# Two buffers for each set of raw expert weights, shared experts first, routing weights before the indexed stores

## Chip, core and metric

One core of a Trainium2 chip runs the whole kernel. The metric is the device time of one execution in microseconds. The engines are TensorE (PE in the rows, its weight loads PEld), VectorE (DVE), ScalarE (ACT), GpSimd (POOL) and SyncE (SP), which only issues DMAs here.

## What is computed

The input `x` is (2, 1024, 128) in float32: 2048 tokens of 128 channels. An attention block comes first, then a mixture of experts; each has a layer norm before it, a layer norm behind it, and adds its result to `x`. The part that the change touches is the second block:

```
rw = _route(x, gate_w, gate_bias)             # 8 of 64 experts a token, from 4 of 8 groups
expert_out = vmap(_mlp)(Wg, Wu, Wd)           # _mlp: silu(x @ gw.T) * (x @ uw.T) @ dw.T, inner width 88
routed = einsum('eth,te->th', expert_out, rw)
shared = _mlp(x, Sg, Su, Sd)                  # inner width 176
out = routed + shared
```

## The kernel before

The 2048 tokens are four quads of 512. The expert layer treats them in two ways. Quads 2 and 3 (`DENSE`) go through all 64 experts: the 64 x 88 inner rows are cut in 11 rounds of 4 sets of 128 rows (8 rows of each of 16 experts), and a step is one set with one quad. Its six products form gate and up from weights and activations split in a high and a low part (`x_hi`, `x_lo`, `w_hi`, `w_lo`), ACT makes the silu in place, DVE multiplies up by the token's routing weight (`weigh`, L1295) and by the gate (`hidden`, L1305), and one more product (`down`, L1762) adds into the quad's PSUM bank. Quads 0 and 1 (`SPARSE`) are sorted by expert instead: GpSimd writes each token's row to eight slots of a DRAM table `pair_x` with 64 indexed stores of 128 rows (`scatter`, L732; a stage `I` is two of them), TensorE works through the table in a burst of 64 units after round 4, and 64 indexed reads (`gather`, L741) bring the results back during rounds 5 to 10. The shared expert is two steps for each quad, the second one (`is_rest`) of only 48 rows.

The first 16 steps (`FIRST`) are the eight shared ones and round 0. Every engine has a hand-written order of stages for them, `PE_ORDER`, `ACT_ORDER`, `DVE_ORDER` and `POOL_ORDER`, and works strictly in it. The letters that matter: `Z` a step (its gate and up on PE, its silu on ACT, its products on DVE), `D` its down product, `E` and `F` input and routing logits of a quad, `H`, `J`, `I`, `O`, `M` on DVE the choice of groups and experts and the sum of the weights, `M` on POOL the routing weights (`write_route`, L817), `G` and `N` their transpose and their spreading over the 128 rows of a set (L1713, L1728), `X` and `Y` the counting that gives the slots, `R` the split of a set of weights. On POOL `I` is a stage of indexed stores.

Raw expert weights arrive in `w_raw`, one buffer a set. ACT copies the high part (`split_hi`, L985), DVE subtracts for the low part (L1371), and the down product reads the raw buffer. So the next load of a set may be issued only when the last down product of its last round is done:

```
sp.wait_ge(s_whi, n + 1)
wait_w_lo(sp, n)
sp.wait_ge(s_down, last_user(n) + 1)
sp.dma_start(w_raw[:, c, :], w_experts[r, c]).then_inc(s_wl[c], 16)
```

SP issues these loads in order (wait at L619, load at L620), and after each of the first ones three of the 38 late loads (`gu_w`, `down_w`, L604) that the burst needs. A step may begin on PE when the hidden product of the step two before it is done (`s_hid`). PE tells the others of its results by `s_gate`, `s_up` and `s_down`, one increment each a step.

Of the kernel before, what the change touches and what calls it, by code (L numbers as in the profile page):

```python
# [41 lines left out]
P = 128  # L42
# [12 lines left out]
def build(nc, x, w_basis_t, w_v, b_v, w_o_t, b_o, gate_w_t, gate_bias, w_experts, w_shared_up,  # L55
# [39 lines left out]
    with ExitStack() as ctx:  # L95
# [32 lines left out]
        up_w = sb("up_w", [P, 2, 512])  # L128
        y_t = sb("y_t", [P, QUADS, 512])
        x_hi = sb("x_hi", [P, len(DENSE) * 512], F32R)  # L130
        x_lo = sb("x_lo", [P, len(DENSE) * 512], F32R)
        route_w = sb("route_w", [P, SETS, len(DENSE) * 512])
        w_raw = sb("w_raw", [P, SETS, 3 * P])
        w_hi = sb("w_hi", [P, SETS, 2 * P], F32R)
# [81 lines left out]
        down_w = sb("down_w", [HID, E, C])  # L216
        pair_in = sb("pair_in", [P, 4, 4, C])
        pair_xt = sb("pair_xt", [P, 2, 2 * P])
        pair_g = sb("pair_g", [P, 2, UNIT_TILES, HID])
        pair_h = sb("pair_h", [P, 2, UNIT_TILES, HID])  # L220
        pair_ht = sb("pair_ht", [HID, 2, 2 * P])
        pair_out = sb("pair_out", [P, 4, UNIT_TILES, C])
        picked = sb("picked", [P, 3, CHOSEN, C])
# [57 lines left out]
        s_rw = sem("route_w_ready")  # L281
        s_wl = [sem(f"expert_w_loaded{k}") for k in range(SETS)]
        s_shl = sem("shared_w_loaded")
# [78 lines left out]
        def stages(names):  # L362
# [16 lines left out]
        )  # L379
        DVE_ORDER = stages(  # L380
# [4 lines left out]
        )  # L385
        POOL_ORDER = stages(
            "B0 S1 P1 S2 P2 S3 D0 K0 P3 X0 R0 D1 R1 R2 F0 X1 L0 L1 E0 J0 D2 M0 F1 X2 J1 E1 D3 "
            "X3 F2 M1 E2 J2 R3 E3 I0 I1 M2 F3 I2 I3 J3 I4 I5 I6 M3 "
            + " ".join(f"I{n}" for n in range(7, 32))
        )  # L390
# [50 lines left out]

        FIRST = [(q, c, False) for q in SPARSE for c in range(SHARED)]
        for q in DENSE:
            FIRST += [(q, c, False) for c in range(SHARED)]
            FIRST += [(q, c, True) for c in range(SETS)]
        FIRST_STEPS = len(FIRST)
# [24 lines left out]
        DEEP = 4  # L471
        AHEAD = 2
        WD = 2 * P
# [17 lines left out]
        def unit_bank(u):  # L491
# [6 lines left out]
        ACT_TAIL = stages(  # L498
            "Z0 Z1 R2 K7 Z2 Z3 R3 Z4 Z5 Z6 Z7 O0 Z8 Z9 O1 Z10 Z11 P0 Y1 Y2 "
        )  # L500
        DVE_TAIL = stages(
            "Z0 Z1 R2 Z2 K7 Z3 R3 V7 Z4 C0 Z5 Z6 Z7 Z8 S0 Z9 N0 Z10 Z11 O2 N1 N2 "
        )
# [8 lines left out]
        def step_of(r, k):  # L512
            return r * PER_ROUND + STEPS0 + k

        def quad_of(k):
            return DENSE[k % 2]
# [29 lines left out]
        def _(sp):  # L546
# [5 lines left out]
            def load_quad(q):  # L552
# [20 lines left out]
                         w_shared_down[1, own:SROWS]).then_inc(s_shl, 16)  # L573
            for c in range(SETS):
                sp.dma_start(w_raw[:, c, :], w_experts[0, c]).then_inc(s_wl[c], 16)
            sp.wait_ge(s_zero, 1)
# [36 lines left out]

            def reload(r, c):

                n = (r - 1) * SETS + c
                sp.wait_ge(s_whi, n + 1)
                wait_w_lo(sp, n)
                sp.wait_ge(s_down, last_user(n) + 1)  # L619
                sp.dma_start(w_raw[:, c, :], w_experts[r, c]).then_inc(s_wl[c], 16)  # L620

            for r in range(1, BURST_AFTER + 2):
                for c in range(SETS):
                    if (r, c) == (BURST_AFTER + 1, SETS - 1):
                        load_late(len(late))
                        for t in range(ST):
                            sp.wait_ge(s_scat[t], 16 * CHOSEN)
                        for g in range(4):
                            load_pairs(g)
                    reload(r, c)  # L630
                    if (r, c) == (1, 0):
                        sp.wait_ge(s_fill, 16 * (PAIR_TILES // 8))
                        sp.wait_ge(s_rw, SETS * len(DENSE))
                        sp.wait_ge(s_tab, 1)
                        sp.wait_ge(s_ysh, 2)
                        sp.wait_ge(s_down, last_user(0) + 1)
                        sp.wait_ge(s_slots, ST)
                    load_late(3)
            load_pairs(4)
            for u in range(BURST):  # L640
                g = (u + 9) // 2
                if u % 2 == 1 and g < PAIR_TILES // 4:
# [3 lines left out]
                             pair_out[:, u % 4]).then_inc(s_ps[u % 4], 16)  # L646
            for r in range(BURST_AFTER + 2, ROUNDS):
                for c in range(SETS):
                    reload(r, c)
            for t in range(ST):  # L650
# [233 lines left out]
        def _(act):  # L884
# [94 lines left out]
            def split_hi(n):  # L979

                c = n % SETS
                act.wait_ge(s_wl[c], 16 * (n // SETS + 1))
                if n >= SETS:
                    act.wait_ge(s_up, ups_through(last_user(n - SETS)))
                a.copy(w_hi[:, c, :], w_raw[:, c, 0:WD]).then_inc(s_whi, 1)  # L985

# [117 lines left out]
            for r, k in ROUND_STEPS:  # L1104
                gate(k, step_of(r, k))
                if (r, k) in ((1, 0), (1, 4)):
                    turned_shared(k // 4)
                if k % 2 == 1:
                    split_hi(r * SETS + k // 2 + AHEAD)
                if (r, k) == (BURST_AFTER, PER_ROUND - 1):  # L1110
                    burst()
                at = r * PER_ROUND + k
                if at in COMBINE_AT:
                    weigh_pairs(COMBINE_AT[at])
            for what, k, _ in ACT_TAIL:
# [20 lines left out]
                elif what == "O":  # L1136
                    act.wait_ge(s_down, LAST_S + unit_step(k) + 1)
                    a.copy(y_t[:, DENSE[k], :], ps[:, acc_bank(DENSE[k]), :]).then_inc(s_yt, 1)

        @block.vector  # L1140
        def _(dve):
# [224 lines left out]
            def split_lo(n):  # L1366

                c = n % SETS
                dve.wait_ge(s_whi, n + 1)
                dve.wait_ge(s_up, ups_through(last_user(n - SETS)))  # L1370
                tt(w_lo[:, c, :], w_raw[:, c, 0:WD], w_hi[:, c, :],  # L1371
                   ALU.subtract).then_inc(s_wlo, 1)
# [120 lines left out]
            for r, k in ROUND_STEPS:  # L1493
                s = step_of(r, k)
                weigh(k, s, quad_of(k), k // 2)
                hidden(k, s)
                if k % 2 == 1:
                    split_lo(r * SETS + k // 2 + AHEAD)
                if (r, k) == (BURST_AFTER, PER_ROUND - 1):
                    burst()  # L1500
                at = r * PER_ROUND + k
                if at in COMBINE_AT:
                    combine(COMBINE_AT[at])
                if at in FINISH_AT:
                    finish(FINISH_AT[at])

            for what, k, _ in DVE_TAIL:
# [10 lines left out]
                elif what == "C":  # L1518

                    dve.wait_ge(s_wl[SETS - 1], 16 * ROUNDS)  # L1520
                    rows = w_raw[:, SETS - 1, WD:WD + P]
                    link(v.bn_stats(wc_stats[:], rows))
# [3 lines left out]
                elif what == "O":  # L1526

                    dve.wait_ge(s_down, LAST_S + unit_step(k))
                    dve.wait_ge(s_yt, k)
                    rest = y_t[:, QUADS - 1, 256:512]  # L1530
                    tt(rest, ps[:, 6, 0:256], rest, ALU.add).then_inc(s_yt, 1)
# [24 lines left out]
        def _(pe):  # L1556
# [408 lines left out]
            def dense_down(s):  # L1965

                if s < FIRST_STEPS:
                    first_down(s)
                else:
                    k = (s - STEPS0) % PER_ROUND  # L1970
                    down(s, quad_of(k), w_raw[:, k // 2, :], P)

# [37 lines left out]
            for what, k, _ in PE_TAIL:  # L2010
# [5 lines left out]
                elif what == "D":  # L2016
# [5 lines left out]
                    else:  # L2022
                        q, c, lo, w = LAST[kd]
                        if lo and c == 0:
                            pe.wait_ge(s_po, BURST)
                        down(LAST_S + kd, q, w_raw[:, c, :], P, start=(lo > 0 and c == 0),
                             stop=(c == SETS - (2 if lo else 1)), lo=lo, w=w)
                elif what == "T":
# [5 lines left out]
                    for t in range(n):  # L2034
                        mm = t_.matmul(ps[:, unit_bank(k), P * t:P * t + P],
                                       y_t[:, q, P * (first + t):P * (first + t) + P], center[:],
                                       start=k + 1 < len(UNITS) or t == 0, stop=True,
# [45 lines left out]
```

## Time and profile before

| | us |
|---|---|
| median of 3 runs (495.16 to 499.41) | 496.69 |
| the profiled execution | 497.04 |
| its span | 495.3 |
| PE busy in the span | 403.5 |
| POOL busy in the span | 184.1 |

The span reaches from the first to the last recorded instruction; 1.7 us lie around it. In rows of a timeline the columns are start, duration, engine, line, operation with its tiles, count, and in brackets how long the engine sat idle before it and who ended that. "issue" there means that the profile shows nothing that the engine waited for, "remote" that the releaser is unknown.

### The profile page before, as it was taken

To read this page: it belongs to the slowest core of one execution; us is meant where nothing else is said; L and a number is where in the kernel's file an instruction comes from. 1 tells how busy PE (TensorE), PEld (TensorE's weight loads), DVE (VectorE), ACT (ScalarE), POOL (GpSimd) and SP (SyncE) were. 2 spreads that over 40 slices of the span, in tenths; PEclk is the share of its full clock that TensorE was granted. 3 is DMA by queue.
4 is the path that set the end of the run, shared out by engine and by line. 5 is a ranking of instruction groups with operands and counts; after the bars stand their busy time and mean duration, and the time that the engine had idled before them with its cause. 6 is when DMAs were issued, how large, how long until landed. Compare 5 with 4: busy or idle time off the path is not lost.

```text
span 495.3 us, 7318 instructions
## 1 busy us (share of the span) xinstructions
PE 403.5 (81%) x2024; PEld 304.3 (61%) x2024; DVE 289.2 (58%) x761; ACT 213.3 (43%) x557; POOL 184.1 (37%) x242
## 2 busy tenths in 40 slices
PE   6889888297631339999969999999994999999985
PEld 5779754153421226666638999999862655555564
DVE  6667876344120126776734666665471888888885
ACT  4769963032110113332325666666533344444533
POOL 7664563657777720000000000000065566767201
PEclk9999988569757668999989999999999799999999
DMA  6088000111141427678144666665322222222211
GB/s 183 16 342 338 1 1 6 38 32 37 54 132 50 130 74 244 186 142 143 48 118 123 181 175 177 171 190 164 109 65 63 74 74 83 82 82 79 60 54 42
DMA packets 65467, 54.03 MB, mean 109 GB/s; under 512 B 7013, under 2 KB 61333, under 8 KB 65429
## 3 DMA queue, kind: packets, MB, share of 16 engines
q1 hardware_dynamic: 60469, 44.85, 31.0%
q0 software_dynamic: 4096, 8.40, 5.8%
q10 hardware_dynamic: 864, 0.33, 0.3%
q8 instruction: 18, 0.29, 0.2%
q14 instruction: 20, 0.16, 0.1%
HBM read 31.53 MB, written 22.02 MB: 108 GB/s over the span
## 4 chain that ended last, share of the span: by engine, by line
PE 45%; another core or an unknown queue 25%; DVE 10%; issue 9%; SPq 4%; ACT 2%; POOL 2%; DMA 1%; POOLq 0%; DVEq 0%; ACTq 0%
PE ps L1762 9%; PE ps L1935 8%; PE ps L1960 6%; PE ps L1733 5%; PE ps L1735 5%; PE ps L1734 5%; SPq L578 4%; PE ps L1913 3%; PE ps L1947 3%; DVE up_w L1295 3%; DVE hid L1305 2%; DVE picked L1409 1%; ACT picked L1082 1%; POOL xn L802 1%
## 5 line engine op out<-in xcount | busy, mean ns | idle before, releaser
L1733 PE MATMUL ps<-x_hi,w_hi 128*128 128x512 f32 (+1 forms) x184 | 101.5, 552 | 53.6 <-issue 37.4
L741 POOL DMA_INDIRECT picked<-pair_y,slots x64 | 62.4, 974 | 202.7 <-DMA pair_y<-pair_out 184.2
L991 ACT ACTIVATE ps<-ps 128x512 f32<-128x512 f32 (+1 forms) x92 | 51.7, 563 | 115.9 <-PE ps L1735 97.5
L1295 DVE TENSOR_TENSOR up_w<-ps,route_w 128x512 f32<-128x512 f32 (+1 forms) x92 | 61.1, 664 | 69.1 <-PE ps L1735 30.4
L1762 PE MATMUL ps<-hid,w_raw 128*128 128x512 f32 (+1 forms) x182 | 94.1, 600 | 1.4 <-DVE hid L1305 1.4
L1733 PEld LDWEIGHTS ps<-x_hi,w_hi 128*128 128x128 f32 x184 | 36.8, 200 | 89.0 <-issue 64.3
L1735 PE MATMUL ps<-x_hi,w_lo 128*128 128x512 f32 (+1 forms) x184 | 74.2, 403 | 0.0
L1734 PE MATMUL ps<-x_lo,w_hi 128*128 128x512 f32 (+1 forms) x184 | 74.1, 403 | 0.0
L732 POOL DMA_INDIRECT pair_x<-x_rows,slots x64 | 62.3, 973 | 21.9 <-issue 18.8
L1305 DVE TENSOR_TENSOR hid<-ps,up_w 128x512 f32<-128x512 f32 (+1 forms) x92 | 61.5, 668 | 6.2 <-ACT ps L991 2.3
L1935 PE MATMUL ps<-gu_w,pair_xt 128*128 x256 | 49.4, 315 | 0.0
L1734 PEld LDWEIGHTS ps<-x_lo,w_hi 128*128 128x128 f32 x184 | 37.3, 203 | 18.7 <-issue 14.0
L1388 DVE COPY pair_ht<-ps 88x256 f32<-88x256 f32 x64 | 26.9, 420 | 37.4 <-PE ps L1947 30.8
L1735 PEld LDWEIGHTS ps<-x_hi,w_lo 128*128 128x128 f32 x184 | 37.0, 201 | 8.2
L1762 PEld LDWEIGHTS ps<-hid,w_raw 128*128 128x128 f32 x182 | 35.4, 200 | 10.3 <-DVE hid L1305 2.3
L1960 PE MATMUL ps<-down_w,pair_ht 88*128 x256 | 39.2, 275 | 0.1
L1935 PEld LDWEIGHTS ps<-gu_w,pair_xt 128*128 128x128 f32 x256 | 38.3, 190 | 1.1 <-issue 0.8
L1371 DVE TENSOR_TENSOR w_lo<-w_raw,w_hi 128x256 fp32r<-128x256 f32 x40 | 16.8, 419 | 34.4 <-issue 31.3
L985 ACT CAST w_hi<-w_raw 128x256 fp32r<-128x256 f32 x44 | 17.5, 399 | 44.5 <-DMA w_raw<-in_w_experts 25.4
L1960 PEld LDWEIGHTS ps<-down_w,pair_ht 88*128 88x128 f32 x256 | 33.6, 191 | 0.3 <-issue 0.3
L1022 ACT COPY pair_out<-ps 128x256 f32<-128x256 f32 x64 | 23.9, 373 | 22.8 <-PE ps L1960 22.8
L1913 PE MATMUL ps<-ident,pair_in 128*128 128x128 f32 x128 | 25.0, 276 | 4.2 <-DMA pair_in<-pair_x 3.7
(221 smaller groups left out, 592.8 us busy)
## 6 DMA issues: line engine op xcount, KB each, us to landing
w_raw<-in_w_experts SPq DMA_DIRECT2D x44, 192.0 KB
pair_x<-zero SPq DMA_DIRECT2D x16, 512.0 KB, 5.6
pair_in<-pair_x SPq DMA_DIRECT2D x32, 256.0 KB, 3.0
pair_y<-pair_out SPq DMA_DIRECT2D x64, 128.0 KB, 2.2
gu_w<-in_w_experts SPq DMA_DIRECT2D x22, 256.0 KB
down_w<-in_w_experts SPq DMA_DIRECT2D x16, 176.0 KB
pair_x<-x_rows,slots POOLq DMA_INDIRECT x64
picked<-pair_y,slots POOLq DMA_INDIRECT x64
```

The source lines that it names most:

```text
L732: g.indirect_dma_start(pair_x, bass.IndirectOffsetOnAxis(ap=slots[:, t, k:k + 1], axis=0), x2_rows[:, t, :], None).then_inc(s_scat[t], 16)
L741: g.indirect_dma_start(picked[:, t % 3, k, :], None, pair_y, bass.IndirectOffsetOnAxis(ap=slots[:, t, k:k + 1], axis=0)).then_inc(s_pick[t ...
L991: a.activation(bank, bank, ACT.Silu).then_inc(s_gated, 1)
L1295: v.tensor_tensor(up_w[:, k % 2, 0:w], ps[:, gate_bank(k) + 1, 0:w], route_w[:, group, 512 * dense_at(q) + lo:512 * dense_at(q) + lo + w], ...
L1305: v.tensor_tensor(hid[:, s % DEEP, 0:w], ps[:, gate_bank(k), 0:w], up_w[:, k % 2, 0:w], ALU.mult).then_inc(s_hid, 1)
L1733: t_.matmul(out_, hi, mhi, start=start, stop=False)
L1734: t_.matmul(out_, hi, mlo, start=False, stop=False)
L1735: return t_.matmul(out_, lo, mhi, start=False, stop=stop)
L1762: t_.matmul(ps[:, acc_bank(q) if lo == 0 else 6, 0:w], weights_[0:n, WD:WD + P], hid[0:n, s % DEEP, 0:w], start=start, stop=stop).then_inc ...
L1913: mm = t_.transpose(ps[:, 4, P * t:P * t + P], pair_in[:, g % 4, 2 * (u % 2) + t, :], ident[:])
L1935: mm = t_.matmul(ps[:, 2 + u % 2, 256 * t:256 * t + 2 * HID], pair_xt[:, u % 2, P * t:P * t + P], own[:, :, :, 0:PACK], start=True, stop=True)
L1960: mm = t_.matmul(ps[:, pair_bank(u), P * t:P * t + P], pair_ht[:, u % 2, P * t:P * t + P], rows[:, bass.ds(at[t], C)], start=True, stop=True)
```

## The change

The first 16 steps are put in another order: the shared steps of all four quads first (steps 0 to 7), then round 0 of quad 2 (8 to 11) and of quad 3 (12 to 15). `w_raw` has eight buffers instead of four, a load is issued two rounds ahead of its use instead of one, and the first eight loads are issued at the start. The splits run three sets ahead instead of two. On POOL and DVE the routing of quad 3 comes earlier: before, seven stages of indexed stores (14 DMAs) stood ahead of `M3`, now two (4 DMAs), and the other 60 follow it without a stage between them. To make room, `y_t` shrinks to two quads and six buffers of the burst share their place with `picked` and `total`.

```
-        w_raw = sb("w_raw", [P, SETS, 3 * P])
+        w_raw = sb("w_raw", [P, 2 * SETS, 3 * P])
...
-            "E1 T34 F1 T35 C31 T36 Z0 T37 C32 C33 Z1 D0 E2 F2 D1 Z2 X0 E3 F3 Z3 D2 X1 Z4 D3 X2 "
-            "Z5 G2 D4 X3 N20 D5 N21 Z6 Z7 D6 Z8 D7 Z9 D8 Z10 D9 Z11 D10 G3 D11 N30 N31 Z12 Z13 "
+            "E1 T34 F1 T35 C31 T36 Z0 T37 C32 C33 Z1 D0 E2 F2 D1 Z2 X0 E3 F3 Z3 X1 D2 Z4 X2 D3 "
+            "Z5 G2 D4 Z6 X3 N20 D5 N21 Z7 Z8 D6 G3 Z9 D7 Z10 D8 N30 D9 N31 Z11 Z12 D10 Z13 D11 "
...
-            "I1 L1 O1 Z1 U3 X3 M1 F2 H2 Y0 Z2 J2 Y1 Z3 I2 O2 M2 Y2 F3 G2 H3 Z4 Y3 Z5 J3 Z6 Z7 "
-            "I3 O3 M3 Z8 Z9 Z10 G3 Z11 Z12 R4 Z13 Z14 R5 Z15 "
+            "I1 L1 O1 Z1 U3 X3 M1 F2 H2 Y0 Z2 J2 F3 Y1 Z3 H3 I2 O2 M2 Y2 J3 Z4 G2 Y3 Z5 I3 O3 "
+            "M3 Z6 Z7 Z8 G3 Z9 Z10 Z11 Z12 Z13 R4 Z14 R5 Z15 R6 "
...
-            "X3 F2 M1 E2 J2 R3 E3 I0 I1 M2 F3 I2 I3 J3 I4 I5 I6 M3 "
-            + " ".join(f"I{n}" for n in range(7, 32))
+            "X3 F2 M1 E2 J2 R3 E3 F3 I0 M2 J3 I1 M3 "
+            + " ".join(f"I{n}" for n in range(2, 32))
...
-        FIRST = [(q, c, False) for q in SPARSE for c in range(SHARED)]
-        for q in DENSE:
-            FIRST += [(q, c, False) for c in range(SHARED)]
-            FIRST += [(q, c, True) for c in range(SETS)]
+        FIRST = [(q, c, False) for q in range(QUADS) for c in range(SHARED)]
+        FIRST += [(q, c, True) for q in DENSE for c in range(SETS)]
...
-            "Z0 Z1 R2 Z2 K7 Z3 R3 V7 Z4 C0 Z5 Z6 Z7 Z8 S0 Z9 N0 Z10 Z11 O2 N1 N2 "
+            "Z0 Z1 R3 Z2 K7 Z3 V7 Z4 C0 Z5 Z6 Z7 Z8 S0 Z9 N0 Z10 Z11 O2 N1 N2 "
...
+            def reload(n):
+                old = n - 2 * SETS
+                sp.wait_ge(s_whi, old + 1)
+                wait_w_lo(sp, old)
+                sp.wait_ge(s_down, last_user(old) + 1)
+                sp.dma_start(w_raw[:, n % (2 * SETS), :], w_experts[n // SETS, n % SETS]
+                             ).then_inc(s_wl[n % (2 * SETS)], 16)
...
-                    split_hi(r * SETS + k // 2 + AHEAD)
+                    split_hi(r * SETS + 3 + k // 2)
```

## Rows read from the trace of the kernel before

**Rows 1.** The page, busy tenths in 40 slices of the span.

```profile
PE   6889888297631339999969999999994999999985
...
POOL 7664563657777720000000000000065566767201
```

**Rows 2.** Five windows: busy time of each engine, clock, DMA share, GB/s.

```profile
81.00:104.00 23.00, 11.80 (x33) 5.42 (x32) 10.93 (x56) 3.74 (x7) 12.81 (x14) 0.62 0.08 26
104.00:129.00 25.00, 21.49 (x67) 13.74 (x66) 11.23 (x28) 7.65 (x14) 16.59 (x19) 0.87 0.13 42
129.00:186.00 57.00, 17.88 (x45) 10.91 (x44) 7.68 (x13) 4.72 (x10) 36.70 (x38) 0.67 0.30 92
186.00:254.00 68.00, 67.21 (x236) 44.77 (x236) 46.42 (x76) 22.26 (x45) 0.00 (x0) 0.98 0.57 140
```

**Rows 3.** The timeline of PE, 130 to 186 us.

```profile
130.30 1.02 PE L1762 MATMUL ps<-hid,w_raw 128*128 128x512 f32 x2
144.66 0.77 PE L1733 MATMUL ps<-x_hi,w_hi 128*128 128x512 f32 x1 [13.34 <-issue]
...
149.77 0.39 PE L1735 MATMUL ps<-x_hi,w_lo 128*128 128x512 f32 x1
150.00 1.02 PE L1762 MATMUL ps<-hid,w_raw 128*128 128x512 f32 x2
164.87 0.80 PE L1733 MATMUL ps<-x_hi,w_hi 128*128 128x512 f32 x1 [13.85 <-issue]
...
178.35 0.76 PE L1733 MATMUL ps<-x_hi,w_hi 128*128 128x512 f32 x1 [8.76 <-issue]
...
185.87 0.80 PE L1733 MATMUL ps<-x_hi,w_hi 128*128 128x512 f32 x1 [3.17 <-DVE hid L1305]
```

**Rows 4.** The timeline of SP's queue: the first and the third reload.

```profile
139.75 0.33 SPq L620 DMA_DIRECT2D w_raw<-in_w_experts  x1
...
182.44 0.34 SPq L620 DMA_DIRECT2D w_raw<-in_w_experts  x1
```

**Rows 5.** The timelines of ACT and DVE in the same stretch.

```profile
142.22 0.40 ACT L985 CAST w_hi<-w_raw 128x256 fp32r<-128x256 f32 x1 [15.69 <-DMA w_raw<-in_w_experts]
...
176.78 0.69 DVE L1295 TENSOR_TENSOR up_w<-ps,route_w 128x512 f32<-128x512 f32 x1 [11.97 <-remote]
```

**Rows 6.** The timeline of POOL: the 50 stores behind M3.

```profile
112.50 1.04 POOL L817 TENSOR_TENSOR route<-left,winv 128x512 f32<-128x512 f32 x1 [3.38 <-DVE winv L1271]
113.70 1.01 POOL L732 DMA_INDIRECT pair_x<-x_rows,slots  x1 [0.16 <-issue]
...
176.01 0.96 POOL L732 DMA_INDIRECT pair_x<-x_rows,slots  x1 [0.30 <-issue]
```

**Rows 7.** The timelines of POOL, PE and DVE, first 16 indexed reads.

```profile
361.18 0.99 POOL L741 DMA_INDIRECT picked<-pair_y,slots  x1 [184.20 <-DMA pair_y<-pair_out]
...
380.06 0.95 POOL L741 DMA_INDIRECT picked<-pair_y,slots  x1 [0.30 <-issue]
...
371.29 0.39 PE L1735 MATMUL ps<-x_hi,w_lo 128*128 128x512 f32 x1
...
373.53 0.39 PE L1735 MATMUL ps<-x_hi,w_lo 128*128 128x512 f32 x1
...
369.49 0.69 DVE L1295 TENSOR_TENSOR up_w<-ps,route_w 128x512 f32<-128x512 f32 x1 [0.82 <-issue]
...
374.64 0.69 DVE L1295 TENSOR_TENSOR up_w<-ps,route_w 128x512 f32<-128x512 f32 x1 [3.41 <-PE ps L1735]
...
383.09 0.69 DVE L1295 TENSOR_TENSOR up_w<-ps,route_w 128x512 f32<-128x512 f32 x1 [7.03 <-remote]
```

**Rows 8.** The timelines of DVE and POOL: routing of quad 2.

```profile
86.66 0.18 DVE L1271 RECIPROCAL winv<-wsum 128x4 f32<-128x4 f32 x1
...
89.70 1.06 POOL L817 TENSOR_TENSOR route<-left,winv 128x512 f32<-128x512 f32 x1
```

**Rows 9.** The timeline of PE in the last round.

```profile
475.22 0.50 PE L1733 MATMUL ps<-x_hi,w_hi 128*128 128x512 f32 x1 [1.33 <-DVE w_lo L1371]
```

More of the change, by code:

```diff
@@ L128, in build @@
         up_w = sb("up_w", [P, 2, 512])
-        y_t = sb("y_t", [P, QUADS, 512])
+        y_t = sb("y_t", [P, 2, 512])
         x_hi = sb("x_hi", [P, len(DENSE) * 512], F32R)
@@ L216, in build, with sb_during @@
         down_w = sb("down_w", [HID, E, C])
[L217 to L222, printed above, removed]
+        during = ExitStack()
+        def sb_during(name, shape):
+            return during.enter_context(nc.sbuf_tensor(name, shape, F32))
+        pair_in = sb_during("pair_in", [P, 4, 4, C])
+        pair_xt = sb_during("pair_xt", [P, 2, 2 * P])
+        pair_g = sb_during("pair_g", [P, 2, UNIT_TILES, HID])
+        pair_h = sb_during("pair_h", [P, 2, UNIT_TILES, HID])
+        pair_ht = sb_during("pair_ht", [HID, 2, 2 * P])
+        pair_out = sb_during("pair_out", [P, 4, UNIT_TILES, C])
+        during.close()
         picked = sb("picked", [P, 3, CHOSEN, C])
@@ L281, in build @@
         s_rw = sem("route_w_ready")
-        s_wl = [sem(f"expert_w_loaded{k}") for k in range(SETS)]
+        s_wl = [sem(f"expert_w_loaded{k}") for k in range(2 * SETS)]
         s_shl = sem("shared_w_loaded")
@@ L471, in build @@
         DEEP = 4
-        AHEAD = 2
         WD = 2 * P
@@ L498, in build @@
         ACT_TAIL = stages(
-            "Z0 Z1 R2 K7 Z2 Z3 R3 Z4 Z5 Z6 Z7 O0 Z8 Z9 O1 Z10 Z11 P0 Y1 Y2 "
+            "Z0 Z1 R3 K7 Z2 Z3 Z4 Z5 Z6 Z7 O0 Z8 Z9 O1 Z10 Z11 P0 Y1 Y2 "
         )
         DVE_TAIL = stages(
-            "Z0 Z1 R2 Z2 K7 Z3 R3 V7 Z4 C0 Z5 Z6 Z7 Z8 S0 Z9 N0 Z10 Z11 O2 N1 N2 "
+            "Z0 Z1 R3 Z2 K7 Z3 V7 Z4 C0 Z5 Z6 Z7 Z8 S0 Z9 N0 Z10 Z11 O2 N1 N2 "
         )
@@ L513, in step_of, with raw_of @@
             return r * PER_ROUND + STEPS0 + k
+        def raw_of(r, c):
+            return (r * SETS + c) % (2 * SETS)
         def quad_of(k):
@@ L573, in _ @@
                          w_shared_down[1, own:SROWS]).then_inc(s_shl, 16)
-            for c in range(SETS):
-                sp.dma_start(w_raw[:, c, :], w_experts[0, c]).then_inc(s_wl[c], 16)
+            for n in range(2 * SETS):
+                sp.dma_start(w_raw[:, n, :], w_experts[n // SETS, n % SETS]).then_inc(s_wl[n], 16)
             sp.wait_ge(s_zero, 1)
@@ L612, in load_pairs @@
                              ).then_inc(s_pin[g % 4], 16)
[L614 to L638, printed above, removed]
+            def reload(n):
[5 more added lines that the diff above has]
+                             ).then_inc(s_wl[n % (2 * SETS)], 16)
+            BEFORE = (BURST_AFTER + 3) * SETS
+            for n in range(2 * SETS, BEFORE):
+                if n == BEFORE - 1:
+                    load_late(len(late))
+                    for t in range(ST):
+                        sp.wait_ge(s_scat[t], 16 * CHOSEN)
+                    for g in range(4):
+                        load_pairs(g)
+                reload(n)
+                if n == 2 * SETS:
+                    sp.wait_ge(s_fill, 16 * (PAIR_TILES // 8))
+                    sp.wait_ge(s_rw, SETS * len(DENSE))
+                    sp.wait_ge(s_tab, 1)
+                    sp.wait_ge(s_ysh, 2)
+                    sp.wait_ge(s_slots, ST)
+                load_late(3)
             load_pairs(4)
@@ L646, in _ @@
                              pair_out[:, u % 4]).then_inc(s_ps[u % 4], 16)
-            for r in range(BURST_AFTER + 2, ROUNDS):
-                for c in range(SETS):
-                    reload(r, c)
+            for n in range(BEFORE, ROUNDS * SETS):
+                reload(n)
             for t in range(ST):
@@ L981, in split_hi @@
                 c = n % SETS
-                act.wait_ge(s_wl[c], 16 * (n // SETS + 1))
+                load = n % (2 * SETS)
+                act.wait_ge(s_wl[load], 16 * (n // (2 * SETS) + 1))
                 if n >= SETS:
                     act.wait_ge(s_up, ups_through(last_user(n - SETS)))
-                a.copy(w_hi[:, c, :], w_raw[:, c, 0:WD]).then_inc(s_whi, 1)
+                a.copy(w_hi[:, c, :], w_raw[:, load, 0:WD]).then_inc(s_whi, 1)
             def gate(k, s, w=512):
@@ L1137, in _ @@
                     act.wait_ge(s_down, LAST_S + unit_step(k) + 1)
-                    a.copy(y_t[:, DENSE[k], :], ps[:, acc_bank(DENSE[k]), :]).then_inc(s_yt, 1)
+                    a.copy(y_t[:, k, :], ps[:, acc_bank(DENSE[k]), :]).then_inc(s_yt, 1)
         @block.vector
@@ L1370, in split_lo @@
                 dve.wait_ge(s_up, ups_through(last_user(n - SETS)))
-                tt(w_lo[:, c, :], w_raw[:, c, 0:WD], w_hi[:, c, :],
+                tt(w_lo[:, c, :], w_raw[:, n % (2 * SETS), 0:WD], w_hi[:, c, :],
                    ALU.subtract).then_inc(s_wlo, 1)
@@ L1497, in _ @@
                 if k % 2 == 1:
-                    split_lo(r * SETS + k // 2 + AHEAD)
+                    split_lo(r * SETS + 3 + k // 2)
                 if (r, k) == (BURST_AFTER, PER_ROUND - 1):
@@ L1518, in _ @@
                 elif what == "C":
-                    dve.wait_ge(s_wl[SETS - 1], 16 * ROUNDS)
-                    rows = w_raw[:, SETS - 1, WD:WD + P]
+                    load = (ROUNDS * SETS - 1) % (2 * SETS)
+                    dve.wait_ge(s_wl[load], 16 * len(range(load, ROUNDS * SETS, 2 * SETS)))
+                    rows = w_raw[:, load, WD:WD + P]
                     link(v.bn_stats(wc_stats[:], rows))
@@ L1529, in _ @@
                     dve.wait_ge(s_yt, k)
-                    rest = y_t[:, QUADS - 1, 256:512]
+                    rest = y_t[:, dense_at(DENSE[1]), 256:512]
                     tt(rest, ps[:, 6, 0:256], rest, ALU.add).then_inc(s_yt, 1)
@@ L1970, in dense_down @@
                     k = (s - STEPS0) % PER_ROUND
-                    down(s, quad_of(k), w_raw[:, k // 2, :], P)
+                    down(s, quad_of(k), w_raw[:, raw_of((s - STEPS0) // PER_ROUND, k // 2), :], P)
             def burst(lagged):
@@ L2025, in _ @@
                             pe.wait_ge(s_po, BURST)
-                        down(LAST_S + kd, q, w_raw[:, c, :], P, start=(lo > 0 and c == 0),
+                        down(LAST_S + kd, q, w_raw[:, raw_of(ROUNDS - 1, c), :], P, start=(lo > 0 and c == 0),
                              stop=(c == SETS - (2 if lo else 1)), lo=lo, w=w)
@@ L2035, in _ @@
                         mm = t_.matmul(ps[:, unit_bank(k), P * t:P * t + P],
-                                       y_t[:, q, P * (first + t):P * (first + t) + P], center[:],
+                                       y_t[:, dense_at(q), P * (first + t):P * (first + t) + P], center[:],
                                        start=k + 1 < len(UNITS) or t == 0, stop=True,
```

4 rows, old and new, of the table ACT_ORDER are left out of this document.

## Prediction

> **What bounds the kernel now.** I read the page's slices first. TensorE is busy at 9 tenths nearly everywhere, and the one long hole, slices 11 to 15, lies where POOL is busy at 7 tenths with nothing but indexed stores [rows 1]. The windows give its size: of 57 us from 129 to 186, TensorE works 17.88, while from 186 to 254 it works 67.21 of 68 [rows 2]. In the full stretch a step takes 2.24 us (236 products, eight passes a step, in 67.21 us: 2.28). The hole is four idle gaps of 13.34, 13.85, 8.76 and 3.17 us, 39.1 in all [rows 3], with four steps between them: step 15 and steps 0, 1, 2 of round 1.
>
> The plain reading of the gaps is a loop through SP: ACT sits 15.69 us at the cast of a reloaded set, for a load that SP issued at 139.75, and behind this cast stand the silu of the next steps, hence `s_hid`, hence TensorE [rows 4, 5]. Two buffers cut this loop. But the reload itself was late for no work: it waits for the down product of step 12, whose second pass ends at about 131.3 [rows 3], and SP goes on 8.4 us later. The third reload waits for the down product begun at 150.00, ended by 151.1, and is issued at 182.44, 31 us later [rows 3, 4]. DVE does the same without SP: at 176.78 it takes step 0 of round 1, whose up product ended at 150.2, and the profile names no releaser [rows 3, 5]. What is late is the news of TensorE's results, not the results.
>
> The same thing happens once more, with no reload in it. Sixteen indexed reads start at 361.18, 1.25 us apart. DVE reads the up product promptly at 369.49; the next one ends at 371.68 and is read at 374.64, the one that ends at 373.92 is read at 383.09 [rows 7]. Later batches of reads are only eight long and show no such lag. In both places the lag sets in after some ten unbroken indexed DMAs (about 10 us into the reads; about 14 us behind the 113.70 of the stores, since TensorE's starts are regular until 130.30) and goes a few microseconds after the last one (381.0 to 383.1; 177.0 to 183.8, when all waiting engines start together) [rows 5 to 7]. I take it so: in a long unbroken run of indexed DMAs TensorE's increments reach the others slowly, one at a time. From 129 to 182.44 nine get through, from the gate of step 14 to the down product begun at 150.00, three a step: 6 us each. That is why four steps take 57 us.
>
> **The change, part by part**, against the profiled execution's own 497.04 us (0.35 above the median).
>
> *Before the slow stretch.* From 81 to 129 TensorE is idle 48 - 11.80 - 21.49 = 14.7 us [rows 2], waiting for routing weights and their helpers. Quad 2's weight sum is ready at 86.84, but POOL writes the routing weights only at 89.70, since four indexed stores lie ahead; now two do, and they can be issued before the sum is there [rows 8]. Quad 3's shared steps, 3.5 us of products, fill what remains, and `M3`, at 112.50 before [rows 6], comes after fewer steps. Following the new orders with the old durations, I get `M3` at about 99, step 8 at about 101 and some 5 us of idle (3 to 8). Gain: 14.7 - 5 = 10 us (7 to 12). The sigmoid, group scores and group choice of quad 3 now stand ahead of quad 2's `I2`, about 3 us of DVE; they run while POOL issues `I0`, and quad 2's sum still comes at about 87.
>
> *The stores.* Before, 14 of the 64 lay ahead of `M3`, broken by other work, and 50 ran unbroken from 113.70 to 177.0, one each 1.27 us [rows 6]. Now 60 run unbroken: 60 x 1.265 = 75.9 us, from about 99.5 to 175.5. The lag should set in 13.5 us into the run, at 113, and its tail of 6.8 us after 50 stores should be about 8 after 60, so TensorE is free at about 185.5, as it is now (185.87). The slow stretch is then 72.5 us instead of 57. It starts with step 11 done instead of step 14. Nine increments passed in 53 us, with a pause in which none was under way (below); some five more pass in the added 15 us, and the two-deep lead of TensorE over the hidden product is kept, so I expect 6.5 steps in it (5 to 8). Loss in the stretch before: 57 - 4 x 2.24 = 48.0. After: 72.5 - 6.5 x 2.24 = 57.9. So 9.9 us are given back (6.5 to 13, and 3.5 more if the lag sets in at 10 us as in the reads).
>
> *Two buffers.* In the slow stretch they take the loop away but not the lag. From 139.7, when SP hears of step 12, to 146.3 no increment was under way, so at most two are gained; that is in the 6.5 steps. Behind it, TensorE's starts from 185.87 run at 2.24 us but for about 1 us, and in 186 to 254 it is idle under 1 us [rows 2]: 1.5 us to gain, no more. The Trainium skill, page "Trainium Kernel Development and Optimization", section "Best Practices", says to double-buffer so that DMA and compute overlap. By that rule the ACT wait of 15.69 us would be the prize; the row of 182.44 speaks against it, since the load there waits for news and not for bandwidth.
>
> *The rest.* The splits a set earlier take the 1.33 us wait for `w_lo` out of the last round [rows 9]; DVE is nearly full there, so 1.3 is the upper end. Four loads more at the start are issued at about 10 us, where SP next waits for a zeroed tile; they cost nothing unless they hold up the clearing of `pair_x`, which nobody waits for before the stores. SP's queue keeps its order: each reload waits for the same down product as before, and the late loads behind it come no earlier. Moving six burst buffers under `picked` adds no wait, since the reads begin when all of the burst is stored. The added stage of ACT and DVE (`R6`) takes the place of one in round 1. Zero, 1 us either way.
>
> Sum: -10 + 9.9 - 1.5 - 1.3 = -2.9, or 494.1; with the median 0.35 lower I say **494.0**. With the bounds of the terms: 488 to 501.
>
> **The rivals.**
>
> *The loop through SP is the cause.* Then the late increments are a sign of idle engines, not a cause, and the two buffers take the whole hole away: 57 us shrink to the 9 of four steps, -48, and with -10 and -2.8 the time is about 436; if half of the lag stays, about 465. For it: the ACT and DVE rows that wait for a load or a split. Against it: DVE's wait to 176.78 and the reads, where no reload is missing [rows 5, 7]. It decides if TensorE's starts stay 2.24 us apart beyond 20 us of unbroken stores. I give the whole effect 0.12 and the half, 455 to 480, 0.16.
>
> *The longer run costs more than it spares.* The lag grows along the run, 8.4 us at 139.75 and 31 at 182.44, so the ten stores more may let nothing through. If the 72.5 us hold no more steps than the 57 of before, four, the loss is 72.5 - 9 = 63.5, which is 15.5 more than now; with the lag setting in at 10 us, 3.5 more. 497.0 - 10 + 15.5 + 3.5 - 2.8 = 503. It decides below 4.7 steps. Chance 0.22.
>
> *It does not do what it says.* `M3` waits for DVE's sum in any case (3.38 us of idle ahead of it [rows 6]); if DVE's chain keeps it at about 112, the order of the stores moves the run 10 us back and the earlier steps fill it: 497. Chance 0.05.
>
> **How the numbers follow.** The forecast has 0.45. The range takes in the slower rival with its bound and the upper part of the halved lag, and leaves out the whole effect (0.12) and a few hundredths on either side: 467 to 507. About 1% is what a measurement of this kernel can tell from no change: 491.7 to 501.7. Faster by more: 0.28 of the rivals and 0.09 of the forecast's lower end, 0.37. Slower by more: 0.19 of the slower rival and 0.01, 0.20. Within: 0.43.
>
> **What would show it.** The windows: TensorE's idle in 81 to 113 falls to about 5 us. POOL: the route of quad 3 at about 99, then stores to about 175. DVE and SP rows with "remote" ahead of them appear from about 113 on, still in the stores, with 5 to 7 steps of TensorE until 185. ACT's casts of `w_hi` no longer wait for a load. The prediction is wrong if the steps go on at 2.24 us during the stores, or if the lag follows something other than an unbroken run of indexed DMAs.

## The result, and the profile after

The changed kernel takes 503.2 us (median of 4 runs, 501.97 to 505.16), the kernel before 498.05 in the same series (495.16 to 499.99). The ratio is 1.0106, 95% interval 1.0068 to 1.0145: slower by 1%. The profiled execution took 503.65 us (span 501.9), 6.6 more than the one of before. That is the time of the rival "The longer run costs more than it spares" (503), not of the forecast (494).

The slices of the page have the hole where they had it, in slices 11 to 15, and it is deeper from its first slice on, 3 tenths for 6 [rows 1]:

```profile
PE   6989878597303049999969999999997799999995
...
POOL 7664554377777700000000000000056466767301
```

The windows of the changed kernel, as in [rows 2] (busy time of PE, PEld, DVE, ACT, POOL, then clock, DMA share, GB/s):

```profile
81.00:104.00 23.00, 17.18 (x50) 9.68 (x49) 14.35 (x72) 6.28 (x11) 11.76 (x13) 0.80 0.05 17
104.00:129.00 25.00, 17.68 (x51) 10.48 (x49) 6.22 (x9) 5.16 (x9) 18.90 (x21) 0.84 0.16 52
129.00:186.00 57.00, 13.04 (x24) 7.41 (x24) 5.98 (x10) 3.09 (x7) 35.74 (x38) 0.56 0.19 59
186.00:254.00 68.00, 67.73 (x241) 45.67 (x242) 45.81 (x76) 22.36 (x47) 0.00 (x0) 0.97 0.65 165
```

The first stretch gained 5.4 us of TensorE's work. The second already lost 3.8, the third 4.8. POOL's timeline, which answers to [rows 6], has the routing weights of quad 3 and then the first and last of 60 unbroken stores:

```profile
99.35 1.04 POOL L822 TENSOR_TENSOR route<-left,winv 128x512 f32<-128x512 f32 x1 [5.63 <-DVE winv L1277]
100.54 1.00 POOL L737 DMA_INDIRECT pair_x<-x_rows,slots  x1 [0.16 <-issue]
...
175.07 0.96 POOL L737 DMA_INDIRECT pair_x<-x_rows,slots  x1 [0.30 <-issue]
```

TensorE's timeline, beside [rows 3], shows the starts of steps 8, 11, 14, 15, 16 and 17:

```profile
101.34 0.63 PE L1740 MATMUL ps<-x_hi,w_hi 128*128 128x512 f32 x1
...
115.33 0.76 PE L1740 MATMUL ps<-x_hi,w_hi 128*128 128x512 f32 x1 [2.35 <-ACT route_w L981]
...
132.41 0.77 PE L1740 MATMUL ps<-x_hi,w_hi 128*128 128x512 f32 x1 [7.91 <-DVE hid L1311]
...
154.22 0.77 PE L1740 MATMUL ps<-x_hi,w_hi 128*128 128x512 f32 x1 [17.20 <-DVE hid L1311]
...
176.51 0.77 PE L1740 MATMUL ps<-x_hi,w_hi 128*128 128x512 f32 x1 [17.69 <-DVE hid L1311]
...
186.27 0.80 PE L1740 MATMUL ps<-x_hi,w_hi 128*128 128x512 f32 x1 [5.94 <-DVE hid L1311]
```

Steps 14 to 16 start 22 us apart. Before, it was step 19 that began at 185.87 [rows 3]; now it is step 17 at 186.27. Those two steps and 0.4 us are 2 x 2.24 + 0.4 = 4.9 of the 6.6 us lost. The waits of 113 to 186 (us in total, times, longest) name no load:

```profile
ACT ps L997 <- remote: 64.3, 4, 21.5
PEld ps L1740 <- issue: 50.4, 5, 19.2
PE ps L1740 <- DVE hid L1311: 42.8, 3, 17.7
DVE up_w L1301 <- remote: 38.6, 3, 20.3
```

Read backwards, the chain is: TensorE waits for DVE's hidden product, DVE and ACT wait ("remote") for the news of gate and up products that ended long before. No cast of `w_hi` waits for a load any more, which [rows 5] had at 15.69 us, and the hole is there all the same. SP's first reload, at 139.75 in [rows 4], comes when the stores are over:

```profile
181.96 0.33 SPq L626 DMA_DIRECT2D w_raw<-in_w_experts  x1
```

The reads lag as in [rows 7]: the 1st, the 16th, the 17th and the last one of POOL.

```profile
367.84 0.98 POOL L746 DMA_INDIRECT picked<-pair_y,slots  x1 [191.82 <-DMA pair_y<-pair_out]
...
386.69 0.94 POOL L746 DMA_INDIRECT picked<-pair_y,slots  x1 [0.30 <-issue]
...
395.78 1.08 POOL L746 DMA_INDIRECT picked<-pair_y,slots  x1 [0.19 <-issue]
...
467.32 0.94 POOL L746 DMA_INDIRECT picked<-pair_y,slots  x1 [0.30 <-issue]
```

The first read is 6.7 us later than before's (361.18 [rows 7]), and from there to the end of the span both kernels take 134.1. So the whole loss lies before the burst's end.

### The profile page after: what moved, and what is told of

Read it like the earlier page. It is cut to its first block, busy times and chain, and to the rows that moved or that the text cites. A ratio compares the mean times of both kernels' runs of the same rounds, so it can differ in the third digit from the quotient of the medians.

```text
span 501.9 us, 7313 instructions
## 1 busy us (share of the span) xinstructions
PE 407.3 (81%) x2024; PEld 306.5 (61%) x2024; DVE 289.0 (58%) x761; ACT 212.7 (42%) x557; POOL 183.1 (36%) x242
## 4 chain that ended last, share of the span: by engine, by line
PE 55%; DVE 13%; issue 12%; another core or an unknown queue 10%; POOL 5%; ACT 3%; DMA 1%; DVEq 0%; POOLq 0%; SPq 0%; ACTq 0%
PE ps L1769 11%; PE ps L1942 8%; PE ps L1742 7%; PE ps L1740 7%; PE ps L1741 6%; PE ps L1967 6%; PE ps L1920 3%; PE ps L1954 3%; DVE up_w L1301 3%; DVE hid L1311 2%; PE ps L1692 2%; POOL xn L807 1%; POOL rstd L776 1%; DVE stats L1165 1%
## 5 line engine op out<-in xcount | busy, mean ns | idle before, releaser
L1769 PE MATMUL ps<-hid,w_raw 128*128 128x512 f32 (+1 forms) x182 | 96.0, 611 | 0.6 <-DVE hid L1311 0.6
L1021 ACT ACTIVATE pair_g<-ps 128x176 f32<-128x176 f32 x64 | 20.3, 317 | 15.9 <-PE ps L1942 15.8
L1012 ACT COPY pair_xt<-ps 128x256 f32<-128x256 f32 x64 | 24.2, 378 | 6.5 <-PE ps L1920 6.5
```

Of the source, the lines that this page charges most:

```text
L1769: t_.matmul(ps[:, acc_bank(q) if lo == 0 else 6, 0:w], weights_[0:n, WD:WD + P], hid[0:n, s % DEEP, 0:w], start=start, stop=stop).then_inc ...
```

## The experiments

They ran on seven occasions, and the kernel before ran on each. On five it took 454.5 to 456.1 us (medians), on two 498.0 and 499.4, as in the series above. The lag is what the prediction read in the rows of before: TensorE's increments of `s_gate`, `s_up` and `s_down` reach the other engines many microseconds late. An occasion where the kernel before takes about 498 is called one with the lag here, the others are without it. Within one occasion the two never mixed. Line numbers shift by a few where an edit adds lines.

### Without the lag

**Pauses between the stores.** In `scatter`, ahead of each stage of two stores from the eighth on, in the kernel before:

```
+                if n >= 7:
+                    pool.wait_ge(s_hid, 10 + (n - 7) * 4 // 3)
```

and from the third on in the changed one:

```
+                if n >= 2:
+                    pool.wait_ge(s_hid, 8 + (n - 2) * 4 // 3)
```

> The kernel before, but each stage of two indexed stores from I7 on first waits for a hidden product of the dense steps (three stages for every four steps of 2.24 us, so one store in 1.49 us instead of 1.27, with pauses). If TensorE's increments lag because of a long unbroken run of indexed DMAs, no lag builds up, the four gaps of 39 us from 131 to 186 all but go, and the time is 455 to 465. If the loop through the reload of the single weight buffer is the cause, the gaps stay and the time is 495 to 500.

> The changed kernel with the same pacing for I2 to I31. Lag theory: the slow stretch from 123 to 186 goes, and what the new order spared ahead of it stays: 448 to 460, a few us under the kernel before with pacing. Rival, that the changed order of steps itself is what makes it slower: it stays 3 to 7 us above the kernel before with pacing.

Measured: before, paced, 456.55 against 456.08 (ratio 1.001, 0.998 to 1.004). Changed, paced, 434.49 (ratio 0.953, 0.947 to 0.959). There was no hole to remove, since the kernel before took 456 itself, so neither run tests the pauses. What they show is that the pauses cost nothing.

**The change in its two halves.** Buffers only: the changed kernel with before's `FIRST` and before's four orders. Orders only: before, with the new `FIRST` and orders, and one buffer a set. In both, the splits `R4` to `R6` stand where the number of buffers wants them.

> The kernel before with the two buffers a set and the splits three sets ahead, but its old order of steps and stores. Lag theory: the stretch from 129 to 184 is set by how fast increments get through, at most two of them are won, 494 to 500. Reload theory: the hole goes, below 465.

> The kernel before with the new order of the first 16 steps and of the stores, but one buffer a set. Lag theory: the run of 60 unbroken stores costs more steps than the run of 50, and the loop through the reload costs one or two increments more: 501 to 508. Reload theory: the loop stays and the idle time ahead of it goes: about 488 to 492.

Measured against 456.08: buffers only 445.37 (0.977, 0.971 to 0.983), orders only 447.45 (0.980, 0.972 to 0.987). That is -10.7 and -8.6 us, together -19.3.

**Both kernels unedited, and before without its stores.** The latter leaves out the 64 indexed stores; SP waits for the slots in their place.

```
-                for k in (2 * half, 2 * half + 1):
+                for k in ():
...
-                            sp.wait_ge(s_scat[t], 16 * CHOSEN)
+                            sp.wait_ge(s_slots, t + 1)
```

> The changed kernel itself, unedited, beside the kernel before. The last chip ran the kernel before in 456 us and no lag of TensorE's increments showed in any trace there, not even in an unbroken run of 60 stores. If that chip was free of the lag: on such a chip the changed kernel is at 434 to 438, 4 to 5% faster (the paced one had 434.5), and on a chip with the lag it is again 1% slower, at about 503 to 498. If the lag came with the kernels and not with the chip, it is at 500 or more here whatever the kernel before does.

> The kernel before without its 64 indexed stores (the routed part of quads 0 and 1 then comes from a table that holds only zeros); nothing else is left out. On a chip with the lag: the hole goes but for the reload loop, 498 to about 457. On a chip without it: the loop alone is left, so within 4 us of the kernel before.

> The kernel before, unedited, for its trace on another chip than the first. On a chip without the lag: the gaps of TensorE from 129 to 186 are not gone but short, four or so of 2 to 5 us, each behind a cast that waits for a reloaded set; time 455. On a chip with the lag the trace of before comes back, 498.

Measured: the changed kernel 435.13 against 455.5 (0.955, 0.950 to 0.959), 20.4 us faster, where the first series had it slower. Without stores 451.69 (0.992, 0.989 to 0.995). Before again, in its own profile, 456.63. The windows of before, 129 to 186:

```profile
129.00:186.00 57.00, 49.28 (x174) 32.69 (x173) 32.13 (x53) 16.02 (x33) 37.36 (x40) 0.94 0.73 211
```

and of the changed kernel:

```profile
129.00:186.00 57.00, 57.00 (x210) 38.39 (x209) 38.72 (x63) 19.61 (x41) 37.81 (x39) 1.00 0.80 231
```

POOL issues the same stores in the same unbroken run, and TensorE works 49.28 and 57.00 us beside them instead of 17.88 and 13.04. What before still loses is the loop through SP. Its two gaps on PE:

```profile
138.31 0.77 PE L1733 MATMUL ps<-x_hi,w_hi 128*128 128x512 f32 x1 [5.16 <-DVE hid L1305]
...
147.58 0.50 PE L1733 MATMUL ps<-x_hi,w_hi 128*128 128x512 f32 x1 [2.41 <-DVE hid L1305]
```

and the two casts on ACT that lead to them:

```profile
135.86 0.40 ACT L985 CAST w_hi<-w_raw 128x256 fp32r<-128x256 f32 x1 [7.51 <-DMA w_raw<-in_w_experts]
...
145.34 0.40 ACT L985 CAST w_hi<-w_raw 128x256 fp32r<-128x256 f32 x1 [8.10 <-DMA w_raw<-in_w_experts]
```

With orders only it stays; the wait of ACT from 104 to 186:

```profile
ACT w_hi L983 <- DMA w_raw<-in_w_experts: 20.9, 4, 8.2
```

With the two buffers no such wait is left. Double-buffering so that load and work overlap is what the Trainium skill asks for ("Trainium Kernel Development and Optimization", "Best Practices"), and without the lag the runs agree: that wait is gone, and the time is 10.7 us shorter.

One page line tells the occasions apart. The part on DMA issues gives the median time from issue to landing. In the runs without the lag it has one for the indexed stores (before, here):

```profile
pair_x<-x_rows,slots POOLq DMA_INDIRECT x64, 2.3
```

and in those with the lag, the two of the first series among them, it has none (the changed kernel):

```profile
pair_x<-x_rows,slots POOLq DMA_INDIRECT x64
```

The waits tell them apart too. ACT at `ps` or DVE at `up_w` waits for "remote" in every profile with the lag, and in none of the 15 without it.

**The place of `M3`, and the paced kernel again.** The changed kernel with stages `I2` to `I6` put back ahead of `M3`:

```
-            "X3 F2 M1 E2 J2 R3 E3 F3 I0 M2 J3 I1 M3 "
-            + " ".join(f"I{n}" for n in range(2, 32))
+            "X3 F2 M1 E2 J2 R3 E3 F3 I0 M2 J3 I1 I2 I3 I4 I5 I6 M3 "
+            + " ".join(f"I{n}" for n in range(7, 32))
```

> The changed kernel with five stages of indexed stores (ten DMAs, 12.7 us) put back ahead of M3, so that only the place of the routing weights is undone. M3 then comes at about 106 instead of 99.4, and TensorE, which reaches the transpose of quad 3's weights at about 105, waits 2 to 3 us and the steps behind it more: without the lag 437 to 442 instead of 435. With the lag the unbroken run is 50 stores again and begins 7 us later: 498 to 503.

> The changed kernel with paced stores once more, in case this chip has the lag: then 450 to 465 beside 498 of the kernel before. Without the lag 434 to 436 beside 455 again.

Measured: 438.52 (0.961, 0.955 to 0.967), and the paced kernel 434.52, as before. So `M3` ahead of the stores is worth about 438.52 - 434.52 = 4.0 us (3.4 against the 435.13 of the other occasion; the changed kernel itself did not run on this one).

**A third time**, on one more occasion without the lag:

> The changed kernel a third time, to see whether the lag shows again. If the lag belongs to the chip or the occasion, a run where the kernel before takes about 456 us gives 435 us with TensorE busy all 57 us from 129 to 186, and a run where it takes about 497 gives about 503 with some 17 us busy there. If it were a chance of each execution, the two would mix on one chip.

> The changed kernel with each store paced on the hidden products, beside the run above. Without the lag: 434.5 us, as twice before. With the lag (the kernel before at about 497): if an unbroken run of indexed DMAs is what delays TensorE's increments, the pauses let them through, TensorE works over 45 of the 57 us from 129 to 186, and the time is 440 to 460; if the lag has nothing to do with the run's being unbroken, it stays near 503.

Measured: the changed kernel 433.55 against 454.48 (0.954, 0.946 to 0.962), paced 434.01 (0.955, 0.944 to 0.966).

### With the lag

**The changed kernel a fourth time.**

> The changed kernel a fourth time, unedited, once beside the kernel before. If the lag is the property of a chip or an occasion, the pair reads either 456 and 434, with TensorE busy all 57 us from 129 to 186, or 497 and 503, with some 17 us busy there; never 456 and 503.

Measured: 501.66, the kernel before 497.96 beside it. The pattern of the first series is back, on TensorE's timeline too (steps 14, 15, 16):

```profile
138.65 0.76 PE L1740 MATMUL ps<-x_hi,w_hi 128*128 128x512 f32 x1 [9.80 <-issue]
...
161.16 0.76 PE L1740 MATMUL ps<-x_hi,w_hi 128*128 128x512 f32 x1 [17.90 <-DVE hid L1311]
...
182.05 0.76 PE L1740 MATMUL ps<-x_hi,w_hi 128*128 128x512 f32 x1 [16.90 <-DVE hid L1311]
```

**Pauses, and no stores.** The two edits from above.

> The changed kernel with each store paced on the hidden products. If the kernel before takes about 498 us here (the lag is there) and the unbroken run of indexed DMAs is what delays TensorE's increments, TensorE works over 45 of the 57 us from 129 to 186 and the time is 440 to 460; if pauses between the stores do not help, it is 495 to 503. If the kernel before takes about 456 us, it is 434.5, as three times before.

> The kernel before without its 64 indexed stores, the table then holding other data. If the lag is there and the stores cause it, the time falls from about 498 to some 452, the whole hole from 129 to 186 gone but the wait for reloads; the lag in the 64 indexed reads, which stay, may hold back a few us. If the hole stays, the stores are not its cause. If the kernel before takes about 456 us, it is 451.7, as it was.

Measured, on one occasion where the kernel before took 499.42 (497.02 to 502.63): the changed kernel, paced, 442.36 and 452.41 in its two executions; before without its stores 462.43 in its only one. The windows of the two, 129 to 186:

```profile
129.00:186.00 57.00, 55.02 (x197) 36.20 (x196) 37.60 (x62) 19.27 (x40) 34.59 (x37) 1.00 0.79 216
```

```profile
129.00:186.00 57.00, 49.45 (x170) 33.01 (x170) 33.28 (x55) 17.00 (x35) 0.00 (x0) 0.94 0.62 176
```

Without the stores TensorE has its 49 us back, with the reload loop and nothing else missing. (This kernel took 10.7 us more than the 451.69 without the lag, and 9.6 of them lie in the 64 reads, which stay: from the first start to the last they take 101.79 us for 92.17. Most of that is in the eight reads that follow the first 16, so the later batches, which the prediction read as free of the lag, can have it too.) With the stores still there, 37 of them in these 57 us against 38, but with pauses, it works 55.02 against 13.04. POOL's waits over the whole span say how much pause that took:

```profile
POOL pair_x L739 <- DVE hid L1313: 21.6, 12, 5.3
```

Twelve pauses of together 21.6 us; the last store is issued at 196.97 instead of 175.07. One of them can be watched. ACT's timeline has a "remote" of 3.48 us, the beginning of a lag; POOL, which waits for a hidden product of these steps, stops for 4.05 us; in its pause two silus go (161.04, 161.87), and ACT's next wait has its name and nearly its usual length again:

```profile
161.04 0.58 ACT L999 ACTIVATE ps<-ps 128x512 f32<-128x512 f32 x1 [3.48 <-remote]
...
164.25 0.58 ACT L999 ACTIVATE ps<-ps 128x512 f32<-128x512 f32 x1 [1.80 <-PE ps L1744]
```

```profile
158.94 0.95 POOL L739 DMA_INDIRECT pair_x<-x_rows,slots  x1 [0.30 <-issue]
163.94 0.95 POOL L739 DMA_INDIRECT pair_x<-x_rows,slots  x1 [4.05 <-DVE hid L1313]
```

The reads were not paced, and there the lag stays. The 16th and the 17th read of the paced kernel:

```profile
325.88 0.94 POOL L748 DMA_INDIRECT picked<-pair_y,slots  x1 [0.30 <-issue]
...
334.79 1.08 POOL L748 DMA_INDIRECT picked<-pair_y,slots  x1 [0.19 <-issue]
```

8.9 us apart; without the lag it is 2.1 (326.77 and 328.88 in the changed kernel). The starts of the first and of the last read share out what the lag costs, by occasion:

| profiled run | lag | first read | 16th to 17th | last read |
|---|---|---|---|---|
| before | no | 328.12 | 2.1 | 419.88 |
| before | yes | 361.18 | 8.2 | 460.30 |
| changed | no | 307.84 | 2.1 | 399.06 |
| changed | yes | 367.84 | 9.1 | 467.32 |
| changed, paced | yes | 307.01 | 8.9 | 406.00 |

In the stores it costs before 33.1 us and the changed kernel 60.0, in the reads 7.4 and 8.3. The pauses spare all of the first (307.01 against 307.84) and none of the second: 406.00 - 399.06 is 7 us, of the 7 by which the profiled execution, 442.36, lies above the 435.4 of the changed kernel's without the lag. The other execution, 10 us longer, has no profile, and its excess stays unexplained.

**Four more, on an occasion without the lag.** Paced before, the two halves again, and the changed kernel with half the pace (`* 2 // 3` for `* 4 // 3`):

> The kernel before with its stores paced on the hidden products from the eighth stage on. If the lag is there (the kernel before at about 498) and pauses let TensorE's increments through, as they did for the changed kernel (447 against 499), the time is 458 to 470, near the 456.5 that it has without the lag. If it was the changed kernel's two buffers that helped and not the pauses, it stays above 485.

> Two buffers, with the orders of before. With the lag: if it is late news and not the reload loop, the buffers give at most 2 or 3 us, 493 to 498; if the loop is the cause, it falls below 470. Without the lag 445.4, as it was.

> The new orders with one buffer. With the lag: the longer run, begun at an earlier step, costs 15 to 19 us and the earlier work gives 10, so 503 to 508; if the buffers are what loses the time, it is below 498. Without the lag 447.5, as it was.

> The changed kernel with half the pace: a stage of two stores waits for two thirds of a step instead of four thirds, so POOL pauses only once TensorE has fallen far behind. If a pause after each two stores is what prevents the lag, it sets in here and a part of it stays, 455 to 485 where the kernel before takes 498; if it is enough that the stores stop when the steps stop, it is near the 447 of the full pace. Without the lag 435.

Measured against 454.72: 454.53 (1.001, 0.997 to 1.005), 443.57 (0.974, 0.966 to 0.981), 446.56 (0.980, 0.969 to 0.992) and 435.76 (0.956, 0.950 to 0.963). They repeat the numbers without the lag. How the change's loss is shared between its halves with the lag, what pauses do for the kernel before, and how much pause is needed, they could not say.

## Why the prediction was wrong

**What bounds the kernel.** The reading was right for the profile that it was made from: with the lag, late news of TensorE's results makes the hole, and the stores are its cause. With no stores (one buffer a set) and with pauses in them (two buffers) the hole goes. What it could not see is that the lag belongs to the occasion. Without it the same stores in the same run hold up nothing.

**Before the slow stretch, -10.** Right: `M3` at 99.35 for 99, step 8 at 101.34 for 101, TensorE idle 6.3 us from 81 to 113 for about 5, and without the lag the orders alone gave 8.6 and 8.2 us (7 to 12 was the range). The lag sets in a little before 113: ACT takes the second of four products for the routing weights at 111.83, 0.9 us after its end, and step 11 begins at 115.33, where on the third occasion without the lag it begins at 113.45 (step 8 at 101.42).

**The stores, +9.9. This is the step that failed: "some five more pass in the added 15 us", "so I expect 6.5 steps in it".** The stretch is as long as I had it, TensorE free at 186.27 for 185.5. Counted from "step 11 done", five steps begin in it, 12 to 16, and not 6.5. That is one more than the four of before, where I had 2.5 more. (Step 11 was not done at 113, it began at 115.33; but step 14 was not done at 129 before either, it began at 128.84 (row below), so the two counts slip by the same step.) DVE takes the up products of steps 11 to 14 here:

```profile
120.35 0.69 DVE L1301 TENSOR_TENSOR up_w<-ps,route_w 128x512 f32<-128x512 f32 x1 [9.22 <-remote]
...
130.85 0.69 DVE L1301 TENSOR_TENSOR up_w<-ps,route_w 128x512 f32<-128x512 f32 x1 [9.08 <-remote]
...
152.55 0.69 DVE L1301 TENSOR_TENSOR up_w<-ps,route_w 128x512 f32<-128x512 f32 x1 [20.28 <-remote]
...
174.95 0.69 DVE L1301 TENSOR_TENSOR up_w<-ps,route_w 128x512 f32<-128x512 f32 x1 [20.65 <-issue]
```

From 120.35 to 181.96, where SP has the down product of step 12, the increments that get through are gate and up of steps 12, 13 and 14 and the down products of 10, 11 and 12. These are nine, as before from 129 to 182.44, and not nine and five more. From 130.85 on each three of them take 22 us, 7.3 us an increment; in the repeat of the changed kernel with the lag, steps 14 to 16 start 22.5 and 20.9 us apart. The kernel before has the same slow pace late in its run. These are the start of step 14 and SP's second reload, which waits for the down product of step 13:

```profile
128.84 0.47 PE L1733 MATMUL ps<-x_hi,w_hi 128*128 128x512 f32 x1
```

```profile
160.03 0.34 SPq L620 DMA_DIRECT2D w_raw<-in_w_experts  x1
```

From there to 182.44 [rows 4] three increments pass in 22.4 us, 7.5 each, while the first three, from 129 to 139.75, took 3.6 each. The mean of 6 us mixes the quick ones at the start of the lag with the slow ones at its end, and a longer run adds time at the slow end: 15.5 us are two increments. My working did not even keep to its mean, by which 15.5 us hold 2.6; and five more, at three a step, make 5.7 steps of the four before and not 6.5. That the lag grows along the run the prediction had read (8.4 us at 139.75, 31 at 182.44), and it gave this to the rival.

The 1.5 steps and the 0.8 us are 1.5 x 2.24 + 0.8 = 4.1 of the 9.5 us by which the profiled execution missed the sum. Another 0.9 was lost in the working: step 18.5 at 185.5 against step 19 at 185.87 is already 0.8 behind, where -10 + 9.9 says 0.1 ahead. The remaining 4.5 are in the next term.

**Two buffers and the tail, -2.8.** They gave nothing with the lag: the kernel lost 1.7 us more behind the hole (6.6 - 4.9), 4.5 off. The idle time after it did go (0 from 186.27 to 254 for 0.79), and so did the wait for `w_lo` [rows 9], but the lag of the reads took 0.9 us more (9.1 against 8.2), and between the hole and the first read TensorE was busy 1.5 us longer than two steps explain (176.45 against 170.50 and 4.48), which I have not traced further. Without the lag the buffers were worth 10.7 and 11.2 us, since the loop through SP is then what waits.

**The rivals.** "The longer run costs more than it spares" gave 503 for 503.2, with one mistake against another, which is luck. Its -10 + 15.5 + 3.5 puts TensorE 9.0 us behind at the end of the hole, and it was 4.9 behind, since one step passed in the added time where the rival has none; against that it counts 2.8 of gains behind the hole, where 1.7 were lost. By its own mark, below 4.7 steps, five would have favoured the forecast. "The loop through SP is the cause", 436, meets the 435.1 of the occasions without the lag, but not by its mechanism: without the lag the loop is worth 10.7 us of the 62 between 497 and 435 and the orders 8.6, and the 41 between 497 and 456 are the lag itself, which the two buffers do not take away: with it the changed kernel took 502 and 503.

## What to carry to other kernels

Where GpSimd issues dozens of indexed DMAs beside a TensorE pipeline, look for waits named "remote" on the readers of PSUM that begin about ten DMAs into the run and end after the last one. If they are there, let each pair of DMAs wait for the pipeline's own progress. In the changed kernel this cost nothing without the lag (434.01 against 433.55 on one occasion), and with it two executions took 442 and 452 beside 499 of the kernel before; unpaced, on the other two occasions with the lag, it took 502 to 505. And profile the kernel before on a second occasion before choosing what to change: a change that removes one stall can be worth 20 us or cost 5, by whether the lag was there. And time that is added to a stall passes at the pace of its end and not at its mean: look at the last increments, not at the average.

## What was not expected of the hardware

The kernel before takes about 455 us on five occasions and 498 on three (the first series among them), with nothing between, and the executions of an occasion agree. The occasions without the lag bore the chip numbers 14, 1, 14, 14 and 9, two of those with it 14 and 13, so the number alone does not decide it; what does stays open. The indexed DMAs themselves keep their pace in both (1.26 us from one to the next); what slows down is the arrival of TensorE's increments at ACT, DVE and SP, and the profile loses the landings of the indexed DMAs with it. DVE's own increments are prompt in the middle of it: a hidden product begun at 153.27 ends at 153.96, and TensorE starts on it at 154.22. The ends of TensorE's products are modelled in the profile, so whether the increment itself is late or the end of the write before it, the rows cannot tell. Whether it is the breaks or the lower mean rate (60 stores in 95 us for 76) that lets the increments through was not told apart.
